# A two-layer decoder on one core: the order of a pair's sum on TensorE, GpSimd's additions, and the start of a recurrence

## The chip, the core and the metric

The kernel runs on one core of a Trainium2 chip. TensorE (PE) does matrix products and transposes into the PSUM banks, VectorE (DVE), ScalarE (ACT) and GpSimd (POOL) work on tiles of 128 partitions, and each engine goes through its own instructions in the order in which they are written. They wait for one another by semaphores. The metric is the time of one execution on the device in microseconds; less is better. It is given as the median of several runs.

## The reference

Input are x of 8 x 256 x 128 and a context of 8 x 512 x 128, in float32. Six blocks follow on each other, each with a residual and a layer norm:

```python
x = _layernorm(x + _L0_attn_ref(x, ...))    # 16 heads of 8; causal band of 64, relative bias
x = _layernorm(x + _L0_xattn_ref(x, ctx))   # 16 heads of 64; norms, rope on keys
x = _layernorm(x + _L0_ffn_ref(x, ...))     # ternary weights, activations scaled by a global max
x = _layernorm(x + _L1_attn_ref(x, ...))    # recurrence over the 256 positions
x = _layernorm(x + _L1_xattn_ref(x, ctx))   # linear attention, 16 heads of 8
x = _layernorm(x + _L1_ffn_ref(x, ...))     # fp8 quantised input and weights, + bias

# the two that the change touches most
attn = jnp.clip(einsum('bhnd,bhsd->bhns', q, rope(k)) * scale, -11.0, 11.0)
out = einsum('bhns,bhsd->bhnd', softmax(attn), v) @ Wo + bo
def step(state, inp):                       # 256 times
    u_t, sp_t = inp
    state = jnp.tanh(state @ A.T + u_t @ B.T) + sp_t
    return (state, state @ C.T)
```

## The kernel before

**Stages.** In a set-up of about 53 us the weights and the context are loaded and split, and the self attention of batch 0 is computed. The main loop follows: 8 batches, each of 8 pairs of cross-attention heads (p = 0 to 7). Beside a batch's pairs runs the self attention of the next batch, cut in 48 slots, six to a pair. A batch lasts 93 us; the first is shorter (part of its preparation lies in the set-up), as is the last (no self attention beside it). Then comes the quantised FFN's end and the start of the recurrence, the 255 steps of the recurrence with the linear attention of the second layer beside them, and a tail with the fp8 product and the last norm.

**Split numbers.** Matrix products of float32 inputs are made from a high and a low part (fp32r): three matmuls L1803, L1804, L1805 for each. The high part is a cast (L1340, L1342 for the weights' wq and wv in the set-up), the low part the difference (L1349).

**A pair.** The keys are turned by rope on VectorE (`keys_job("a")` makes k_cos, L1312; `keys_job("b")` makes k_sin, L1314) and added on GpSimd (`rotate`, L659, two pairs ahead). `unit(0)` and `unit(1)` on TensorE (L2204) make the scores of the pair in transposed form, half the context each. ScalarE takes the exponential (L1003), VectorE clamps it (`clamp`, L1499), which is the clip of the scores. `values_of` (L2113) multiplies the exponentials with the values. The denominator of the softmax takes two steps: GpSimd adds the four blocks of context positions (L752 when the first clamp is done, L758 and L759 when the second is; L759 gives `psum_ready`), and `sum_of` (L2124) adds over the partitions with a matmul of ones and gives `o_full`. On that VectorE's `attended` waits: a reciprocal (L1399), then the product (L1400). Values, sum and `attended` belong to the pair before.

**The order around the change** is written by hand for each engine. TensorE does unit(0), keys a, a slot, values and sum of the pair before, a slot, unit(1), queries, a slot, keys b, the rest:

```python
if pair >= 1:
    values_of(pair - 1)
    sum_of(pair - 1)
slots(1, 2)
unit(1)
```

VectorE does keys a, clamp(0), two slots, `attended(pair - 1)`, clamp(1), a slot, keys b, the other slots. GpSimd does two slots, L752, L758, L759, three slots, `rotate(pair + 2)`, a slot. Which work stands in which slot is a table: `S_X1` = 37 (the norm of x with b_wo added, L642 to L710) is in pair 6, `S_LATN`, `S_LAT` = 38, 43 make the latents of the next batch (L1187), `S_AFFINE` = (36, 38) multiplies the linear attention's keys by l_g and adds l_b (L696), `S_RELU` = 40 and the k, v product (L1933) follow. TensorE's row maxima for the self attention are made by VectorE (L1248, L1250) from the scores L1819.

**Start of the recurrence.** `begin_z(k)` (L2300, L2301) makes the input part of the first 32 steps for four batches in `cf`, with 256 and 252 columns for each k; step 0 is the first tanh (L1049). `quantize_weights` (L1486, L1487, L1423 to L1427) and the peak `f_peak` (L1557) are on VectorE before. In the steps, matmuls without use (`keep_clock`, L2130) fill TensorE where no other work stands.

**Tail.** `begin_sum(k)` (L2485) puts x5 and b_ffn, both times a diagonal, in a bank; the fp8 product (L2502) is added. ScalarE's `copy_q8` (L1096) brings the turned inputs, `normalize_last` (L1076) applies the last norm with rstd and tail_bias, which GpSimd makes (L818 to L821).

Of the kernel before, what the change touches and what calls it, by code (L numbers as in the profile page):

```python
# [23 lines left out]
ALU = mybir.AluOpType  # L24
# [44 lines left out]
S_AFFINE, S_RELU, S_KV_SUM = (36, 38), 40, 44  # L69
# [116 lines left out]
def decoder(nc, a, out):  # L186
    with ExitStack() as ctx:
# [3 lines left out]
        def sem(name):  # L191
            return ctx.enter_context(nc.semaphore(name))
# [6 lines left out]
        cf = sc[:, :, :].rearrange("p k c -> p (k c)")  # L199
        ob = ctx.enter_context(nc.psum_tensor("out_bank", [P, 512], F32))  # L200
# [130 lines left out]
        f_peak = sb("f_peak", [P, B - 1])  # L331
# [52 lines left out]
        x5_last = sem("x5_last")  # L384
        w_top_ready = sem("w_top_ready")
# [56 lines left out]
        weights_split = sem("weights_split")  # L442
        keys_split = sem("keys_split")
# [168 lines left out]
        def _(pool):  # L612
# [125 lines left out]
            def batch(b, last=False):  # L738

                for p in range(PAIRS):  # L740
# [6 lines left out]
                    slots(0, 2)  # L747
# [8 lines left out]
                    link(first)  # L756
                    pool.wait_ge(clamped, 2 * pair + 2)
# [51 lines left out]
            def affine_of(k, count=4):  # L809
# [9 lines left out]
                link(g.tensor_tensor(rstd[:, at], var_eps[:, at], minus_half[:, at], ALU.pow))  # L819
# [13 lines left out]
            rstd_of(late, 3, 3, EPS_LN, half=1)  # L833
            for k in range(3):
                affine_of(4 + k)
# [8 lines left out]
        def _(act):  # L844
# [127 lines left out]
            even_turn(8)  # L972
            keep_kv(0, 1)
            even_turn(10)
# [141 lines left out]
            copy_q8(2)  # L1116
            normalize_last(0)
            copy_q8(3)
# [4 lines left out]
        def _(dve):  # L1123
# [206 lines left out]
            def split_high(part):  # L1330
# [8 lines left out]
                if part == 2:  # L1339
                    last = w.tensor_copy(wq_s[:, 0, :], wq_nat)  # L1340
                if part == 3:
                    last = w.tensor_copy(wv_s[:, 0, :], wkv_nat[:, INNER:2 * INNER])  # L1342
                last.then_inc(weights_high, 1)

            def split_low(part):

                dve.wait_ge(weights_high, part + 1)
                full, t = ((wq_nat, wq_s), (wkv_nat[:, INNER:2 * INNER], wv_s))[part - 2]
# [19 lines left out]
            split_high(2)  # L1368
# [3 lines left out]
            split_high(3)  # L1372
# [1162 lines left out]
```

## Time and profile before

| | us |
|---|---|
| median of 3 runs | 1004.24 |
| lowest and highest | 1001.86, 1004.31 |
| the profiled execution | 998.63 |
| its span in the trace | 996.9 |
| a batch of the loop (batches 1 to 6) | 93.00 |
| last batch | about 78 |
| end of the loop to step 0 | about 22.5 |
| 255 steps | about 145.5 |
| tail | about 50 |

Over the span TensorE is busy in 908.7 us (91%), VectorE in 687.6 (69%), ScalarE in 504.6 (51%), GpSimd in 501.1 (50%). Of the chain of work that ended last TensorE holds 53% and VectorE 26%. In the timelines a row is a group of like instructions that follow each other, with the start of the first, the time they hold the engine, and in brackets the idle time before them with what ended it. Ends of matmuls are modelled, so the start of the next row says better how long a row took.

### The profile page before, as it was taken

How to read it: one execution, taken by the hardware profiler on the slowest of the kernel's cores; microseconds unless marked ns; L12 is line 12 of the kernel's file. 1: busy time of each engine (PE TensorE's matmuls, PEld its weight loads, DVE VectorE, ACT ScalarE, POOL GpSimd, SP SyncE). 2: the span in 40 equal slices, each digit the busy share in tenths (PEclk: the TensorE clock that was granted, in tenths of full speed). 3: DMA queues.
4: the chain of work that ended last, by engine and by line, in shares of the span. 5: the costliest groups of instructions: out<-in, count | busy, mean ns of one | idle time of the engine just before them, and what ended most of it. 6: DMA issues, size and time to landing. Idle time of an engine off the chain costs nothing.

```text
span 996.9 us, 22201 instructions
## 1 busy us (share of the span) xinstructions
PE 908.7 (91%) x8566; PEld 647.8 (65%) x8566; DVE 687.6 (69%) x1911; ACT 504.6 (51%) x1434; POOL 501.1 (50%) x635
## 2 busy tenths in 40 slices
PE   6679999999999999999999999999899499999944
PEld 4456657666666766666666666666666389998832
DVE  6866578568757875786688567857799735444476
ACT  6456636653764566456646654764243033333324
POOL 2654465367446645664565367456667112333352
PEclk9999999999999999999999999999999689999967
DMA  8000000000000000000000000000000002122111
GB/s 202 23 7 12 1 2 6 12 1 7 12 1 1 7 12 1 1 7 11 2 6 1 12 2 1 1 1 1 23 1 1 0 8 31 32 33 31 30 22 42
DMA packets 60470, 15.09 MB, mean 15 GB/s; under 512 B 41278, under 2 KB 59726, under 8 KB 60238
## 3 DMA queue, kind: packets, MB, share of 16 engines
q1 hardware_dynamic: 59822, 13.42, 6.4%
q8 instruction: 68, 1.11, 0.5%
q14 instruction: 36, 0.29, 0.1%
q10 hardware_dynamic: 544, 0.26, 0.1%
HBM read 10.51 MB, written 3.17 MB: 14 GB/s over the span
## 4 chain that ended last, share of the span: by engine, by line
PE 53%; DVE 26%; POOL 10%; ACT 6%; issue 4%; DMA 1%; POOLq 0%; DVEq 0%; SPq 0%; ACTq 0%
PE score_banks L2204 8%; DVE o_rec L1399 7%; PE out_bank L2113 6%; DVE prob L1499 6%; PE bank_a L1798 4%; PE score_banks L1803 4%; PE score_banks L2325 3%; PE score_banks L2130 3%; PE score_banks L1834 3%; POOL psum L758 3%; PE bank_d L2338 2%; POOL psum L759 2%; PE bank_d L1819 2%; PE score_banks L1804 2%; PE score_banks L1805 2%
## 5 line engine op out<-in xcount | busy, mean ns | idle before, releaser
L1003 ACT ACTIVATE prob<-score_banks 128x1024 f32<-128x1024 f32 x128 | 130.9, 1023 | 161.5 <-PE score_banks L2204 161.1
L758 POOL TENSOR_TENSOR psum<-psum,prob 128x512 f32<-128x512 f32 x63 | 80.4, 1276 | 140.6 <-DVE prob L1499 140.6
L2204 PE MATMUL score_banks<-qh,kr 64*128 64x256 f32 x1024 | 145.2, 402 | 2.8 <-ACT qh L935 1.9
L1399 DVE RECIPROCAL o_rec<-out_bank 128x256 f32<-128x256 f32 x64 | 111.8, 1747 | 23.5 <-PE out_bank L2124 23.4
L752 POOL TENSOR_TENSOR psum<-prob 128x512 f32<-128x512 f32 x64 | 82.6, 1290 | 89.9 <-DVE prob L1499 89.8
L2113 PE MATMUL out_bank<-prob,v 128*64 128x256 f32 x1024 | 124.7, 385 | 0.5 <-DVE on L1400 0.5
L2204 PEld LDWEIGHTS score_banks<-qh,kr 64*128 64x128 f32 x1024 | 88.7, 186 | 39.9 <-issue 30.6
L1499 DVE TENSOR_SCALAR prob<-prob 128x1024 f32<-128x1024 f32 x128 | 101.4, 793 | 12.5 <-ACT prob L1003 12.5
L886 ACT ACTIVATE prob<-prob,neg_max 128x128 f32<-128x128 f32 (+1 forms) x256 | 107.1, 427 | 5.5 <-DVE neg_max L1255 5.5
L2113 PEld LDWEIGHTS out_bank<-prob,v 128*64 128x64 f32 x1024 | 67.7, 136 | 45.8 <-issue 17.2
L1052 ACT ACTIVATE prob<-score_banks 128x8 f32<-128x8 f32 x255 | 45.2, 177 | 93.3 <-PE score_banks L2325 93.3
L759 POOL TENSOR_TENSOR psum<-psum,prob 128x512 f32<-128x512 f32 x63 | 80.3, 1275 | 4.9
L659 POOL TENSOR_TENSOR kr<-k_cos,k_sin 128x512 f32<-128x512 f32 x64 | 81.5, 1273 | 1.8 <-DVE k_sin L1314 1.1
L2325 PE MATMUL score_banks<-prob,pt 128*64 128x8 f32 x1020 | 73.9, 210 | 0.3 <-ACT prob L1049 0.3
L1312 DVE TENSOR_TENSOR k_cos<-score_banks,cos_t 128x512 f32<-128x512 f32 x56 | 38.0, 679 | 44.4 <-PE score_banks L1805 27.2
L854 ACT ACTIVATE pt<-bank_a 128x512 f32<-128x512 f32 x84 | 50.2, 598 | 35.5 <-PE bank_a L1798 34.6
L2325 PEld LDWEIGHTS score_banks<-prob,pt 128*64 128x64 f32 x1020 | 51.5, 135 | 16.1 <-ACT prob L1052 8.4
L2130 PE MATMUL score_banks<-w_qkv_t,ident 128*64 128x96 f32 (+1 forms) x336 | 60.7, 264 | 0.0
L1798 PE MATMUL bank_a<-ident,prob 128*128 128x128 f32 x360 | 56.9, 280 | 4.2 <-ACT pt L854 2.3
L1834 PE MATMUL score_banks<-pt,vm 128*32 128x128 f32 x768 | 54.0, 281 | 5.3 <-ACT pt L940 2.6
L1819 PE MATMUL bank_d<-km,q 64*128 64x128 f32 x480 | 49.2, 322 | 9.1 <-DVE row_max L1250 7.2
L784 POOL TENSOR_TENSOR var_eps<-mv,epsilons 128x1 f32<-128x1 f32 x49 | 10.2, 209 | 93.4 <-DVE mv L1616 93.3
(440 smaller groups left out, 2132.6 us busy)
## 6 DMA issues: line engine op xcount, KB each, us to landing
cb<-in_ctx_dram SPq DMA_DIRECT2D x8, 256.0 KB, 2.8
bias_mask<-bias_scratch SPq DMA_DIRECT2D x4, 384.0 KB, 5.2
xb<-in_x_dram SPq DMA_DIRECT2D x8, 128.0 KB, 2.1
prob<-in_L_xattn_Wkv_dram SPq DMA_DIRECT2D x1, 1024.0 KB, 9.7
x_scratch<-v SPq DMA_DIRECT2D x16, 64.0 KB, 1.5
bias_mask<-x_scratch SPq DMA_DIRECT2D x16, 64.0 KB
att_scratch<-on SPq DMA_DIRECT2D x16, 64.0 KB, 1.5
prob<-att_scratch SPq DMA_DIRECT2D x16, 64.0 KB, 3.0
```

Of the source, the lines that this page charges most:

```text
L758: link(g.tensor_tensor(psum[:, p % 2, :], psum[:, p % 2, :], pp[:, 2, :], ALU.add))
L759: g.tensor_tensor(psum[:, p % 2, :], psum[:, p % 2, :], pp[:, 3, :], ALU.add).then_inc(psum_ready, 1)
L886: last = s.activation(pr, pr, ACT.Exp, bias=neg_max[:, qt, j, g:g + 1], accum_out=row_sum[:, qt, j, g:g + 1])
L1003: s.activation(prob[:, p % 2, 2 * u:2 * u + 2, :].rearrange("p k (h q) -> p h k q", h=2), sc[:, 0:2, :].rearrange("p h (k q) -> p h k q", ...
L1399: link(w.reciprocal(o_rec[:, :], bank[:, T:2 * T]))
L1499: w.tensor_scalar(pr, pr, float(np.exp(-CLIP)), float(np.exp(CLIP)), ALU.max, ALU.min).then_inc(clamped, 1)
L1798: return nc.tensor.transpose(out_ap, in_ap, ident[0:in_ap.shape[0], 0:in_ap.shape[0]])
L1834: last = mm(o0_bank[32 * g:32 * g + 32, qt * P:(qt + 1) * P], vm[:, kt, j, 32 * g:32 * g + 32], pt[:, t % 2, i * P:(i + 1) * P], start=(j ...
L2113: mm(o[DH * h:DH * (h + 1), 0:T], v[:, (q // 2) % 2, kb, lo:lo + DH], prob[:, q % 2, kb, T * h:T * (h + 1)], start=(kb == 0), stop=(kb == ...
L2130: mm(bank[0:HALF_ROWS, 0:columns], ident[:, 0:HALF_ROWS], w_qkv_t[:, 0:columns], start=True, stop=True, skip_group_check=True)
L2204: last = mm(sc[:, h, k * T:(k + 1) * T], kr[rows_of, p % 2, kb * P:(kb + 1) * P], qh[rows_of, p % 2, :], start=True, stop=True, skip_group ...
L2325: last = mm(cf[lo:lo + HALF_ROWS, t * B:(t + 1) * B], a_t[:, lo:lo + HALF_ROWS], hid[:, (t - 1) * B:t * B], start=False, stop=True, skip_g ...
```

## The change

- **Sum.** In each pair TensorE does `sum_of(pair - 1)` behind `unit(1)`, no longer right behind the values.
- **GpSimd.** The multiplication by l_g is in slot 34 (pair 5) instead of 36; in pair 6 the first addition goes ahead of slot 37.
- **Set-up.** The high parts of wv and wq are made by ScalarE; VectorE makes their low parts in other places; keys a of pair 1 come behind the latents' slot.
- **Start of the recurrence.** Before step 0 only the first 16 steps get their input part, in the bank `bank_d2` (`z_of`); the next 16 steps' part is made in steps 1 to 8, by two matmuls in a step (`next_z`), and `keep_clock` gets 96 columns there. `quantize_weights` comes later, the peak is taken by batches.
- **Tail.** For k = 0, 1 GpSimd adds b_ffn to x5 beforehand, and `begin_sum` needs one term. The last three biases are one instruction of VectorE (`bias_of`) in place of two of GpSimd. `copy_q8(3)` comes ahead of `normalize_last(0)`.

```diff
-S_AFFINE, S_RELU, S_KV_SUM = (36, 38), 40, 44
+S_AFFINE, S_RELU, S_KV_SUM = (34, 38), 40, 44
...
# GpSimd, a pair
-                    slots(0, 2)
+                    early = 1 if p == S_X1 // PER_PAIR else 2
+                    slots(0, early)
                     pool.wait_ge(clamped, 2 * pair + 1)
...
                     link(first)
+                    slots(early, 2)
                     pool.wait_ge(clamped, 2 * pair + 2)
...
# ScalarE, set-up
             even_turn(8)
+            act.wait_ge(split_in, 16 * 2)
+            s.activation(wv_s[:, 0, :], wkv_nat[:, INNER:2 * INNER], ACT.Identity).then_inc(values_high, 1)
+            s.activation(wq_s[:, 0, :], wq_nat, ACT.Identity).then_inc(values_high, 1)
+            even_turn(10)
             keep_kv(0, 1)
-            even_turn(10)
...
# VectorE, set-up
             self_attention(0, S_CN_LOW, 0)
-            split_high(2)
             odd_turn(7)
             keep_cos()
             measure_kv(0, 1)
-            split_high(3)
-            split_low(2)
             odd_turn(9)
             invert_sums(0)
             odd_turn(11)
+            split_low(0)
             self_attention(0, S_DIVIDE, 0)
-            split_low(3)
...
             first_keys("b", 0)
+            split_low(1)
             self_attention(0, S_LATN, 0)
+            self_attention(0, S_LAT, 0)
             first_keys("a", 1)
-            self_attention(0, S_LAT, 0)
...
# TensorE, a pair
                     if pair >= 1:
                         values_of(pair - 1)
-                        sum_of(pair - 1)
                     slots(1, 2)
                     unit(1)
+                    if pair >= 1:
+                        sum_of(pair - 1)
...
# TensorE, start of the recurrence
+            pe.wait_ge(y_free, B)
...
-                zv, xv = (t[:, 0:Z_FIRST].rearrange("p (t b) -> p t b", b=B)[:, :, batches] for t in (cf, x3_t))
+                zv, xv = (t[:, 0:P].rearrange("p (t b) -> p t b", b=B)[:, :, batches] for t in (bank_d2, x3_t))
                 mm(zv, bwi_t, xv, start=False, stop=False, skip_group_check=True)
-                return mm(zv[:, 1:], aws_t, xv[:, 0:Z_FIRST // B - 1], start=False, stop=True, skip_group_check=True)
+                return mm(zv[:, 1:], aws_t, xv[:, 0:WINDOW_STEPS - 1], start=False, stop=True, skip_group_check=True)
+
+            def next_z(at):
+
+                k, at = divmod(at, 4)
+                second, half = divmod(at, 2)
+                of = halves[half]
+                batches = slice(4 * k, 4 * k + 4)
+                lag = B if second else 0
+                weights = (bwi_t, aws_t)[second]
+                mm(cf[of, P:Z_FIRST].rearrange("p (t b) -> p t b", b=B)[:, :, batches], weights[:, of],
+                   x3_t[:, P - lag:Z_FIRST - lag].rearrange("p (t b) -> p t b", b=B)[:, :, batches], start=False,
+                   stop=True, skip_group_check=True)
...
# tail: ScalarE, TensorE
             copy_q8(2)
+            copy_q8(3)
             normalize_last(0)
-            copy_q8(3)
...
-                for rhs, first in ((x5[:, 4 * k:4 * k + 4, :], True),
-                                   (b_ffn[:, :].unsqueeze(1).broadcast_to([P, 4, D]), False)):
+                if k < 2:
+                    pe.wait_ge(x5b_ready, k + 1)
+                terms = [((x2, x5)[k // 2][:, 4 * k:4 * k + 4, :], True)]
+                if k >= 2:
+                    terms.append((b_ffn[:, :].unsqueeze(1).broadcast_to([P, 4, D]), False))
+                for rhs, first in terms:
```

The line numbers move: what was L2113, L2124, L2204 and L1803 is L2142, L2153, L2233 and L1831 in the changed kernel. On TensorE, in pair 3 of a batch, before (each row is one instruction with its output and inputs; `x4` means four alike):

```order
776 L1834 MATMUL score_banks<-pt,vm 32x128 x4
777 L2113 MATMUL out_bank<-prob,v 64x256 x8
778 L2124 MATMUL out_bank<-psum,ones 64x256 x2
779 L2204 MATMUL score_banks<-qh,kr 128x256 x4
780 L1803 MATMUL score_banks<-lat_s,wq_s 128x256
```

and in the changed kernel:

```order
776 L1862 MATMUL score_banks<-pt,vm 32x128 x4
777 L2142 MATMUL out_bank<-prob,v 64x256 x8
778 L2233 MATMUL score_banks<-qh,kr 128x256 x4
779 L2153 MATMUL out_bank<-psum,ones 64x256 x2
780 L1831 MATMUL score_banks<-lat_s,wq_s 128x256
```

The sum, out_bank from psum and ones, has gone from between values and scores to behind the scores.

On GpSimd, from pair 5's last two additions to pair 6's, before:

```order
81 L759 TENSOR_TENSOR psum<-psum,prob 128x512
82 L659 TENSOR_TENSOR kr<-k_cos,k_sin 128x512
83 L642 TENSOR_TENSOR var_eps<-mv,epsilons 128x2
84 L644 TENSOR_TENSOR rstd<-var_eps,minus_half 128x2
85 L696 TENSOR_TENSOR k<-k,l_g 128x512
86 L642 TENSOR_TENSOR var_eps<-mv,epsilons 128x2
87 L644 TENSOR_TENSOR rstd<-var_eps,minus_half 128x2
88 L710 TENSOR_TENSOR x<-x,b_wo 128x256
89 L752 TENSOR_TENSOR psum<-prob 128x512
90 L758 TENSOR_TENSOR psum<-psum,prob 128x512
```

and in the changed kernel:

```order
81 L768 TENSOR_TENSOR psum<-psum,prob 128x512
82 L703 TENSOR_TENSOR k<-k,l_g 128x512
83 L666 TENSOR_TENSOR kr<-k_cos,k_sin 128x512
84 L649 TENSOR_TENSOR var_eps<-mv,epsilons 128x2
85 L651 TENSOR_TENSOR rstd<-var_eps,minus_half 128x2
86 L760 TENSOR_TENSOR psum<-prob 128x512
87 L649 TENSOR_TENSOR var_eps<-mv,epsilons 128x2
88 L651 TENSOR_TENSOR rstd<-var_eps,minus_half 128x2
89 L717 TENSOR_TENSOR x<-x,b_wo 128x256
90 L767 TENSOR_TENSOR psum<-psum,prob 128x512
```

The multiplication by l_g stands ahead of the rotation of pair 5, and the first addition of pair 6 (psum from prob alone) ahead of the second rstd and x.

## Rows read from the trace of the kernel before

**Rows 1.** Stages: length, busy PE, PEld, DVE, ACT, POOL, clock, DMA, GB/s
```profile
329.10:422.10 93.00, 89.55 (x693) 60.80 (x692) 67.00 (x175) 53.53 (x136) 51.51 (x53) 1.00 0.02 6
701.00:779.00 78.00, 70.02 (x506) 47.71 (x505) 67.80 (x131) 26.04 (x37) 50.97 (x51) 1.00 0.03 8
779.00:801.50 22.50, 12.91 (x41) 9.16 (x41) 14.73 (x58) 2.83 (x4) 3.82 (x7) 0.58 0.00 0
```

**Rows 2.** Waits of PE, five batches, 220 to 686: total, times, longest
```profile
PE out_bank L2124 <- POOL psum L759: 5.8, 5, 1.2
PE bank_d L1819 <- DVE row_max L1250: 4.2, 5, 0.9
```

**Rows 3.** Waits of DVE in the same stretch
```profile
DVE o_rec L1399 <- PE out_bank L2124: 15.6, 15, 1.4
```

**Rows 4.** Timeline of PE, batch 3, pairs 2 and 3: start, length
```profile
362.68 0.82 PE L1819 MATMUL bank_d<-km,q 64*128 64x128 f32 x8
...
369.20 1.95 PE L2113 MATMUL out_bank<-prob,v 128*64 128x256 f32 x16
370.97 0.60 PE L2124 MATMUL out_bank<-psum,ones 128*64 128x256 f32 x4
371.51 1.13 PE L2204 MATMUL score_banks<-qh,kr 64*128 64x256 f32 x8
372.57 0.39 PE L1803 MATMUL score_banks<-lat_s,wq_s 128*128 128x256 f32 x1
...
376.54 0.38 PE L1803 MATMUL score_banks<-wv_s,cn_s 128*128 128x256 f32 x1 [0.24 <-DVE k_sin L1314]
```

**Rows 5.** Timeline of DVE, batch 3, pairs 1 to 3
```profile
347.73 1.75 DVE L1399 RECIPROCAL o_rec<-out_bank 128x256 f32<-128x256 f32 x1
...
358.66 1.76 DVE L1399 RECIPROCAL o_rec<-out_bank 128x256 f32<-128x256 f32 x1 [0.39 <-PE out_bank L2124]
...
371.62 1.76 DVE L1399 RECIPROCAL o_rec<-out_bank 128x256 f32<-128x256 f32 x1 [1.36 <-PE out_bank L2124]
...
375.81 0.68 DVE L1314 TENSOR_TENSOR k_sin<-score_banks,sin_t 128x512 f32<-128x512 f32 x1
```

**Rows 6.** Timeline of all engines, batch 2, pair 7
```profile
318.94 1.03 ACT L1003 ACTIVATE prob<-score_banks 128x1024 f32<-128x1024 f32 x1 [1.27 <-PE score_banks L2204]
...
319.95 1.58 DVE L1187 TENSOR_SCALAR lat<-x,mv,rstd 128x128 f32<-128x128 f32 x2
320.17 1.28 POOL L758 TENSOR_TENSOR psum<-psum,prob 128x512 f32<-128x512 f32 x1 [0.69 <-DVE prob L1499]
...
322.85 0.65 PE L2124 MATMUL out_bank<-psum,ones 128*64 128x256 f32 x4 [1.17 <-POOL psum L759]
...
324.05 1.48 DVE L1261 TENSOR_SCALAR k<-k 128x512 f32<-128x512 f32 x1 [1.92 <-POOL k L696]
```

**Rows 7.** Timeline of DVE, set-up, 31 to 49
```profile
31.78 1.76 DVE L1340 CAST wq_s<-prob 128x1024 fp32r<-128x1024 f32 x1
...
35.87 0.66 DVE L1342 CAST wv_s<-prob 128x1024 fp32r<-128x1024 f32 x1
36.44 1.22 DVE L1349 TENSOR_TENSOR wq_s<-prob,wq_s 128x1024 fp32r<-128x1024 f32 x1
...
42.47 1.36 DVE L1349 TENSOR_TENSOR wv_s<-prob,wv_s 128x1024 fp32r<-128x1024 f32 x1
...
48.56 0.60 DVE L1187 TENSOR_SCALAR lat<-x,mv,rstd 128x128 f32<-128x128 f32 x2 [0.51 <-POOL rstd L644]
```

**Rows 8.** Timeline before step 0, PE and ACT
```profile
797.80 1.06 PE L2300 MATMUL score_banks<-prob,pt 128*128 128x256 f32 x2
798.05 1.09 ACT L986 ACTIVATE prob<-out_bank 128x512 f32<-128x512 f32 x1 [0.77 <-PE out_bank L1798]
```

**Rows 9.** Timeline of the tail, PE and ACT
```profile
978.41 1.86 PE L2485 MATMUL bank_d<-b_ffn,q 128*128 128x512 f32 x2
...
988.96 0.61 ACT L1096 ACTIVATE q_t<-bank_a 128x512 bf16<-128x512 bf16 x1
```

More of the change, by code:

```diff
@@ L199, in decoder, with z_of @@
         cf = sc[:, :, :].rearrange("p k c -> p (k c)")
+        def z_of(t, count=1):
+            return (bank_d2 if t < WINDOW_STEPS else cf)[:, t * B:(t + count) * B]
         ob = ctx.enter_context(nc.psum_tensor("out_bank", [P, 512], F32))
@@ L330, in decoder @@
         peak = sb("peak", [P, 5])
-        f_peak = sb("f_peak", [P, B - 1])
+        f_peak = sb("f_peak", [P, B])
         tail_bias = sb("tail_bias", [P, 8])
@@ L818, in affine_of @@
                 link(g.tensor_tensor(var_eps[:, at], mv[:, at, 1], eps, ALU.add))
-                link(g.tensor_tensor(rstd[:, at], var_eps[:, at], minus_half[:, at], ALU.pow))
+                last = g.tensor_tensor(rstd[:, at], var_eps[:, at], minus_half[:, at], ALU.pow)
+                if k >= 4:
+                    last.then_inc(rstd_ready, 1)
+                    return
+                link(last)
                 link(g.tensor_tensor(tail_bias[:, at], mv[:, at, 0], rstd[:, at], ALU.mult))
@@ L833, in _ @@
             rstd_of(late, 3, 3, EPS_LN, half=1)
+            pool.wait_ge(red_ready, 3)
+            for k in range(2):
+                part = slice(4 * k, 4 * k + 4)
+                g.tensor_tensor(x2[:, part, :], x5[:, part, :], b_ffn[:, :].unsqueeze(1).broadcast_to([P, 4, D]),
+                                ALU.add).then_inc(x5b_ready, 1)
             for k in range(3):
@@ L1338, in split_high @@
                                              wkv_nat[:, 0:INNER].rearrange(swapped, t=2, d=HALF)[:, 1 - t])
[L1339 to L1342, printed above, removed]
                 last.then_inc(weights_high, 1)
             def split_low(part):
-                dve.wait_ge(weights_high, part + 1)
-                full, t = ((wq_nat, wq_s), (wkv_nat[:, INNER:2 * INNER], wv_s))[part - 2]
+                dve.wait_ge(values_high, part + 1)
+                full, t = ((wkv_nat[:, INNER:2 * INNER], wv_s), (wq_nat, wq_s))[part]
                 w.tensor_tensor(t[:, 1, :], full, t[:, 0, :].bitcast(F32), ALU.subtract).then_inc(weights_split, 1)
@@ L1554, in _ @@
             normalize_f(B - 1)
-            quantize_weights()
+            find_f_peak(B - 2)
             dve.wait_ge(f_t_free, B)
-            link(w.tensor_reduce(f_peak[:, B - 2:B - 1], f_t[:, (B - 2) * T:B * T], AX_X, ALU.max,
+            link(w.tensor_reduce(f_peak[:, B - 1:B], f_t[:, (B - 1) * T:B * T], AX_X, ALU.max,
                                  apply_absolute_value=True))
@@ L1763, in measure_sum, with bias_of @@
                 measure(tiles_of_sum(k), k % 2)
+            def bias_of(k):
+                at = slice(4 * (k % 2), 4 * (k % 2) + 4)
+                dve.wait_ge(rstd_ready, late + 5 + k)
+                w.scalar_tensor_tensor(out=tail_bias[:, at], in0=mv[:, at, 0], scalar=-1.0, in1=rstd[:, at],
+                                       op0=ALU.mult, op1=ALU.mult).then_inc(tail_bias_ready, 1)
             quantize(0)
@@ L1770, in _ @@
             measure_sum(1)
+            bias_of(0)
             measure_sum(2)
+            bias_of(1)
             def measure_tiles(lo, at):
@@ L2324, in step @@
                 for lo in range(0, P, HALF_ROWS):
-                    last = mm(cf[lo:lo + HALF_ROWS, t * B:(t + 1) * B], a_t[:, lo:lo + HALF_ROWS],
+                    last = mm(z_of(t)[lo:lo + HALF_ROWS], a_t[:, lo:lo + HALF_ROWS],
                               hid[:, (t - 1) * B:t * B], start=False, stop=True, skip_group_check=True)
```

32 lines of the change are left out of this document (22 added, 10 removed).

## The prediction

> **What bounds the kernel now.** The view by stages says where the time is: a batch of the main loop lasts 93.00 us and TensorE is busy in 89.55 of it [rows 1]; the other seven batches are like it, except the first (about 76 us, since its early work lies in the set-up) and the last, where TensorE is busy in 70.02 of 78.00 us. So TensorE bounds the loop, and all its gaps in a batch come to 3.4 us. The reader is to see two things in that: no edit that only takes TensorE's gaps away can bring more than 3.4 us a batch, and there is almost no air to take up a delay. The waits of five batches say what ends those gaps: 5.8 us in 5 times at the sum L2124 behind GpSimd's L759, 4.2 us in 5 times at L1819 behind the row maxima [rows 2]. The first is what the change aims at: 1.17 us once per batch, in pair 7. Then I asked the other way round who waits for the sum. VectorE's reciprocal waited 15.6 us in 15 times for L2124 [rows 3], three times per batch. So in three pairs of eight the sum is not an idle appendix of the values, but the step that lets VectorE go on.
>
> The timelines of TensorE and VectorE through batch 3 say what hangs on that. In pair 3 the sum starts at 370.97 and the next scores at 371.51; the reciprocal starts at 371.62 after 1.36 us of idleness, and VectorE then works without a break (reciprocal, product, clamp, four row maxima, their negation, k_sin from 375.81 for 0.68); TensorE's next keys start at 376.54, 0.24 us late, behind that k_sin [rows 4, 5]. The path sum, VectorE, TensorE is therefore the bound there.
>
> **Part 1, the sum behind the second scores.** In each pair but the first, the four sum matmuls go behind unit(1), eight score matmuls. TensorE does them at 371.51 and goes on at 372.57 by the chain of starts, so 1.06 us [rows 4]. Nothing is added to TensorE's work but one more change of tile shape: the sum has the same tiling as the values before it (its four start 0.11 apart, like the values' sixteen in 1.77), and from the sum's start to the scores it is 0.54, 0.10 more than four times 0.11 [rows 4]. The sum now stands between two other tilings, so that change comes once more, and I count 0.15 with the longer first group. The sum ends 1.06 + 0.15 = 1.21 us later against the values.
>
> The Trainium skill has a rule on this ("TensorEngine Tiling (Array Packing)", section Key Properties): changing the tiling mode drains TensorE. The trace agrees with a small price, the 0.10 above; it is a rule that speaks against this order.
>
> By pairs, what is late next:
> - Pair 3: VectorE's chain binds, as shown. It starts 1.21 later, TensorE's wait of 0.24 becomes 1.45: +1.21.
> - Pair 2: the reciprocal starts at 358.66, 0.39 us after VectorE was free, behind the sum; product, clamp and four row maxima follow (in pair 3 the like takes 3.8 from the reciprocal's start), so the maxima end near 362.5, and TensorE's L1819, which needs them, starts at 362.68 [rows 4, 5]. The slack is about 0.15. So +1.06 for the delay less that slack, and 0.15 for the switch, about +1.16.
> - Pair 1: the reciprocal starts at 347.73, when VectorE comes free and not when the sum is done [rows 5]. By the order of the rows the moved sum ends some 0.2 to 0.3 after that, and the chain ends in TensorE's wait of 0.86 at L1819 behind row maxima (4.2 in 5 times [rows 2]), which grows by it: +0.35.
> - Pair 0: as pair 1, but behind the product stand the output matmuls of the batch before, at the end of the pair, which follow at once. I take 0.3 for the delay and 0.15 for the switch, near pair 1's: +0.45.
> - Pairs 4 and 5: the reciprocal comes later, but TensorE does not wait for VectorE soon after; the switch alone, +0.15 each.
>
> **Part 2, GpSimd's order in pairs 5 to 7.** The multiplication by l_g goes from pair 6 into pair 5 ahead of the rotation, and the first addition L752 ahead of the pair-6 slot with x1. In pair 7 the 1.17 us at the sum [rows 6] go: GpSimd comes to its additions earlier, and the sum asks later by 1.06. But what is late next is the latents' normalisation: VectorE's two operations take 1.58 us together from 319.95 while L758 runs on GpSimd from 320.17 to 321.45, against 0.33 for an undisturbed one (the second ends when L758 ends), and the relu that follows took 1.48 from 324.05 under L696 and L659, after a wait of 1.92 for l_b [rows 6]. The k, v product of TensorE waits for that relu. Behind the change the l_g and the first additions meet the same VectorE operations in other places: in pair 5 the rotation is 1.27 later, and k_cos of pair 6 waits for it. I estimate +1.4 for these against −1.17, so +0.2 for pairs 6 and 7 together, with −0.65 if nothing of it blocks.
>
> The page "SBUF — State Buffer" of the Trainium skill (section SBUF: two separate sides) says that VectorE and GpSimd share a port pair that one instruction holds alone to its end. Rows 6 agree: the stretched operations end with GpSimd's.
>
> The sum of a batch: 0.45 + 0.35 + 1.16 + 1.21 + 0.15 + 0.15 + 0.2 = +3.7, bounds +2.3 (pairs 2 and 3 and the switches, pairs 0 and 1 absorbed, −0.65) and +4.2. Six such batches +22.1; batch 0 has no sum in its first pair and less self attention to wait for, +3.1; in the last batch four of the sums release a reciprocal on the path, about +4.1. **Together +29.3**.
>
> **Part 3, the set-up.** Ahead of VectorE's reciprocals of the row sums, three operations leave: 1.76 (wq_s), 0.66 (wv_s), and the low part 1.22; the low part of 1.36 between o and y leaves too [rows 7]. On the other side the wq low part, 1.22, goes in ahead of the latents' normalisation with 0.51 us of idleness as cover [rows 7]. VectorE's chain to the first scores is shorter by 1.76 + 0.66 + 1.22 + 1.36 − 0.71 = 4.3. ScalarE does the two conversions in their place (a 128x1024 operation of it takes 1.03 [rows 6]), in a hole of its own before keep_kv; I charge 0.3. **−4.0**, bounds −2.5 (ScalarE's hole is not where I put it) and −4.6.
>
> **Part 4, the start of the recurrence.** TensorE's four matmul pairs of 256 and 252 columns at half the clock begin at 797.80, 0.85 apart, and become 64 and 60 columns. The second half of them can't begin before ScalarE's copy from 798.05 ends, 1.09 later [rows 8], so 1.5 comes off, not 2.5. The recurrence then starts in the half clock (0.58 granted in that stage [rows 1]); its first eight steps carry the other 384 columns as extra matmuls, about 0.8 us together. f_peak comes 0.57 earlier because the weights' quantisation moves behind, where VectorE waits anyway; this is half lost to ScalarE. **−1.3**, bounds −2.2 and 0.
>
> **Part 5, the tail.** The first of the b_ffn matmul pairs, 1.86 at half the clock [rows 9], goes, but what follows waits for q8; −1.2. copy_q8(3), which stood behind the normalisation until 988.96 [rows 9], comes some 2.8 earlier, the bias path on GpSimd is two operations of 0.20 shorter, but the end then hangs on the statistics and the power on GpSimd in series: −0.3 to −0.7. **−1.5**, bounds −1.9 and +1.0: TensorE gets its full clock back near 980 after a stretch with this very work; with less of it the later matmul pairs may run at 1.2 GHz.
>
> **Sum.** 29.3 − 4.0 − 1.3 − 1.5 = +22.5. The profiled execution took 998.63 us, the median of the three runs is 1004.24, 0.6% above; the change by the sum is the same against either: 1021.1 on the profile's basis, **1026.7** on the median's.
>
> **The rivals.**
> 1. The forecast: the delayed sum is on VectorE's path in pairs 2 and 3 and partly in 0 and 1. Chance 0.68.
> 2. The same mechanism, but pairs 0 and 1 take up their delay and nothing blocks in pairs 6 and 7: +2.3 a batch, over the loop 6 x 2.3 + 2 + 3.5 = +19, less 6.8: 1016. For it speaks that VectorE is busy in only 67.00 of 93.00 us [rows 1]. 0.15.
> 3. The other side: the delay of the sum is taken up everywhere. Place: pair 3's k_sin and pair 2's row maxima. It decides at whether VectorE's chain behind the sum still ends before TensorE gets there; it would have to be 1.2 us shorter, for instance because the product and reciprocal no longer meet GpSimd's operations. Then only the switch costs, 8 x 0.15 = 1.2 a batch, and the wait of 1.17 goes: 0 a batch. The other stages give −6.8, and a part of the L1819 waits may go with it, 2 more: 995 to 997. Against it: the idle 1.36 us before the reciprocal and the idle 0.24 before the keys, with nothing free between [rows 4, 5]. 0.12.
> 4. That the start and the tail lose their clock: the forecast's loop, +3: 1030. 0.05. It is in the range.
>
> **How the numbers follow.** About 0.3%, 3 us, is what a measurement of this kernel can tell from no change. Rivals 1, 2 and 4 are slower by more, 0.68 + 0.15 + 0.05 = 0.88; of rival 3 0.12, faster; between them some lands within 3 us, for which I move 0.04 from the slower side and 0.01 from the faster: faster 0.11, same 0.05, slower 0.84. The range: the forecast's own bounds are +2.3 to +4.2 a batch over eight batches, about +19 to +33, less 8.7 to 2, so 1014 to 1035; with 2 us for the spread of the median the low end is 1012, which leaves out rival 3 and the ends. High 1034.
>
> **What would show it.** In pair 3 of a batch VectorE's idleness before the reciprocal should be about 2.4 (before 1.36 plus the scores), and TensorE's wait at the value keys L1831 (the old L1803) behind k_sin about 1.4, five times in five batches. The sum's wait for GpSimd should be gone. A batch should last about 96.7. The first scores should begin near 48.9 instead of 52.89. I am wrong if a batch lasts 93 or less: then VectorE's chain after the sum was not the bound, or GpSimd's new order gives it more than I see. I am wrong on part 2 if the wait at the k, v product does not show.

## The result, and the profile after

| | before | after |
|---|---|---|
| median (4 runs each) | 1003.05 us | 1024.58 us |
| lowest and highest | 1001.12, 1004.31 | 1023.06, 1026.19 |
| ratio, 95% interval | | 1.0235 [1.0213, 1.0258] |
| the profiled execution | 998.63 | 1025.33 |

The changed kernel is slower by 2.35% in the recorded ratio. Its two medians lie 21.5 us apart, which is 2.15%; in the sets of runs behind the experiments the kernel before had medians of 1000.0 to 1001.3, and against these the change costs 23 to 25 us. The two profiled executions lie 26.7 us apart; that of before is below all its timed runs, and that of after in the upper half of its. By the starts of score rows and of tanh rows the 26.7 us divide like this:

| stretch | before | after | difference |
|---|---|---|---|
| start to the first scores | 52.89 | 49.75 | −3.14 |
| batches 0 to 6 | 648.04 | 673.11 | +25.07 |
| first scores of batch 7 to the last scores' last row | 68.34 | 72.61 | +4.27 |
| from there to the tanh of step 0 | 32.17 | 32.05 | −0.12 |
| 255 steps | 145.53 | 147.78 | +2.25 |
| last tanh to the end | 49.94 | 48.31 | −1.63 |

The loop has lost 29.3 us. The stage view of one batch of after, with the columns of [rows 1], and the start of the recurrence (this second row begins 5.5 us behind the last scores, its counterpart in [rows 1] 9.7 us, so their lengths can't be compared; both end at step 0):

```profile
336.30:432.90 96.60, 90.60 (x691) 60.18 (x690) 66.00 (x174) 54.60 (x136) 52.40 (x53) 1.00 0.02 5
801.00:827.50 26.50, 14.03 (x57) 10.65 (x57) 19.70 (x72) 3.36 (x4) 4.23 (x8) 0.61 0.00 0
```

TensorE is busy in 90.60 us where it was 89.55, and has 6.0 us of gaps where it had 3.4: 1.0 of the 3.6 us that a batch has grown is more busy time of TensorE (eight more changes of tile shape at 0.15 would be 1.2), 2.6 is waiting. What the waiting is for stands in TensorE's waits of five batches (in total, times, longest), and below it VectorE's first row:

```profile
PE bank_d L1847 <- DVE row_max L1274: 9.9, 10, 1.1
PE score_banks L1831 <- DVE k_sin L1338: 6.8, 5, 1.4
PE bank_d L1961 <- DVE k L1285: 5.3, 5, 1.1
PE out_bank L2142 <- DVE on L1418: 1.8, 5, 0.4
```

```profile
DVE o_rec L1417 <- PE out_bank L2153: 48.9, 30, 3.4
```

The sum no longer waits for GpSimd ([rows 2] had 5.8 us for that), but the row maxima have gone from 4.2 us in 5 times to 9.9 in 10, and k_sin from 0.24 a batch to 1.37. VectorE waits 9.8 us a batch for the moved sum, in six pairs, where it waited 3.1 in three [rows 3]. The length of such a wait doesn't say what it costs: the longest, 3.4 us, stands in pair 5, which grew by 0.15, and that of 2.6 in pair 3, which grew by 1.2.

In pair 2 of batch 3 the chain of waits shows one such turn from TensorE to VectorE and back:

```profile
366.19 1.06 PE score_banks L2233 x8
367.25 0.61 PE out_bank L2153 x4
367.86 0.02 issue
367.88 1.77 DVE o_rec L1417
369.65 0.02 issue
369.67 0.42 DVE on L1418
370.10 0.60 DVE prob L1517
...
371.68 0.14 issue
371.82 0.82 PE bank_d L1847 x8
```

Values, scores, sum, reciprocal, product, clamp, row maxima, TensorE: the scores L2233 have come to stand in this chain; before, they ran beside it. In pair 3 the timelines of VectorE and TensorE answer to [rows 5] and [rows 4]:

```profile
381.97 1.76 DVE L1417 RECIPROCAL o_rec<-out_bank 128x256 f32<-128x256 f32 x1 [2.58 <-PE out_bank L2153]
```

```profile
386.88 0.38 PE L1831 MATMUL score_banks<-wv_s,cn_s 128*128 128x256 f32 x1 [1.37 <-DVE k_sin L1338]
```

Idle 2.58 instead of 1.36 before the reciprocal, and 1.37 instead of 0.24 before the keys: about 1.2 more at either end. Pair by pair, from one pair's first scores to the next pair's in batch 3 (starts of the L2204 or L2233 rows in the trace of each kernel):

| pair | 0 | 1 | 2 | 3 | 4 | 5 | 6 | 7 | batch |
|---|---|---|---|---|---|---|---|---|---|
| before | 12.04 | 12.38 | 12.40 | 14.85 | 11.20 | 11.94 | 6.84 | 11.32 | 92.96 |
| after | 12.49 | 12.74 | 13.53 | 16.06 | 10.99 | 12.09 | 6.73 | 12.00 | 96.63 |
| sum's order alone (e1) | 12.49 | 12.74 | 13.54 | 16.04 | 10.98 | 12.09 | 6.73 | 11.73 | 96.33 |
| all but the sum's order (e2) | 12.03 | 12.38 | 12.40 | 14.84 | 11.20 | 11.94 | 6.84 | 10.81 | 92.45 |
| e2 without GpSimd's order (e6) | 12.03 | 12.38 | 12.41 | 14.84 | 11.20 | 11.94 | 6.84 | 11.34 | 92.99 |
| sum moved in pairs 4 to 7 (e4) | 12.04 | 12.39 | 12.40 | 14.84 | 10.99 | 12.08 | 6.73 | 11.99 | 93.47 |
| after, half reciprocal (e3) | 12.02 | 11.95 | 12.73 | 15.27 | 10.98 | 12.09 | 6.73 | 10.90 | 92.67 |
| e2, half reciprocal (e8) | 11.88 | 11.81 | 12.39 | 14.85 | 11.20 | 11.94 | 6.84 | 10.51 | 91.43 |

### The profile page after: what moved, and what is told of

It reads as the page before. It is cut to its first block, busy times and chain, and to the rows that moved or that the text cites. A ratio compares the mean times of both kernels' runs of the same rounds, so it can differ in the third digit from the quotient of the medians.

```text
span 1023.6 us, 22230 instructions
## 1 busy us (share of the span) xinstructions
PE 919.3 (90%) x8580; PEld 647.7 (63%) x8580; DVE 679.5 (66%) x1913; ACT 515.0 (50%) x1436; POOL 508.4 (50%) x631
## 3 DMA queue, kind: packets, MB, share of 16 engines
q8 instruction: 69, 1.13, 0.5%
HBM read 10.51 MB, written 3.17 MB: 13 GB/s over the span
## 4 chain that ended last, share of the span: by engine, by line
PE 60%; DVE 24%; POOL 8%; issue 3%; ACT 3%; DMA 1%; POOLq 0%; DVEq 0%; SPq 0%; ACTq 0%
PE score_banks L2233 10%; DVE o_rec L1417 9%; PE out_bank L2142 8%; PE bank_a L1826 4%; PE score_banks L1831 4%; PE score_banks L2159 3%; PE score_banks L2369 3%; PE score_banks L1862 3%; DVE prob L1517 3%; PE out_bank L2153 3%; PE out_bank L2125 3%; PE bank_d L2382 2%; POOL psum L767 2%; PE bank_d L1847 2%; POOL k L703 2%
## 5 line engine op out<-in xcount | busy, mean ns | idle before, releaser
L767 POOL TENSOR_TENSOR psum<-psum,prob 128x512 f32<-128x512 f32 x63 | 80.6, 1279 | 182.6 <-DVE prob L1517 182.6
L2233 PE MATMUL score_banks<-qh,kr 64*128 64x256 f32 x1024 | 145.5, 402 | 1.6 <-ACT prob L1024 1.0
L2142 PE MATMUL out_bank<-prob,v 128*64 128x256 f32 x1024 | 124.6, 385 | 4.0 <-DVE on L1418 4.0
L2233 PEld LDWEIGHTS score_banks<-qh,kr 64*128 64x128 f32 x1024 | 88.4, 186 | 39.0 <-issue 29.1
L2142 PEld LDWEIGHTS out_bank<-prob,v 128*64 128x64 f32 x1024 | 67.7, 136 | 49.8 <-issue 14.7
L1517 DVE TENSOR_SCALAR prob<-prob 128x1024 f32<-128x1024 f32 x128 | 87.7, 685 | 3.6 <-ACT prob L1024 3.6
L1073 ACT ACTIVATE prob<-score_banks 128x8 f32<-128x8 f32 x240 | 42.7, 178 | 87.0 <-PE score_banks L2369 87.0
L2369 PE MATMUL score_banks<-prob,pt 128*64 128x8 f32 x960 | 69.3, 210 | 0.0
L947 ACT ACTIVATE v<-score_banks 128x512 f32<-128x512 f32 x57 | 34.1, 598 | 67.5 <-PE score_banks L1833 66.8
L793 POOL TENSOR_TENSOR var_eps<-mv,epsilons 128x1 f32<-128x1 f32 x49 | 10.4, 211 | 93.1 <-DVE mv L1635 93.0
L2369 PEld LDWEIGHTS score_banks<-prob,pt 128*64 128x64 f32 x960 | 48.3, 134 | 12.9 <-ACT prob L1073 6.5
```

Source lines behind the costliest of these rows:

```text
L767: link(g.tensor_tensor(psum[:, p % 2, :], psum[:, p % 2, :], pp[:, 2, :], ALU.add))
L1517: w.tensor_scalar(pr, pr, float(np.exp(-CLIP)), float(np.exp(CLIP)), ALU.max, ALU.min).then_inc(clamped, 1)
L2142: mm(o[DH * h:DH * (h + 1), 0:T], v[:, (q // 2) % 2, kb, lo:lo + DH], prob[:, q % 2, kb, T * h:T * (h + 1)], start=(kb == 0), stop=(kb == ...
L2233: last = mm(sc[:, h, k * T:(k + 1) * T], kr[rows_of, p % 2, kb * P:(kb + 1) * P], qh[rows_of, p % 2, :], start=True, stop=True, skip_group ...
L2369: last = mm(z_of(t)[lo:lo + HALF_ROWS], a_t[:, lo:lo + HALF_ROWS], hid[:, (t - 1) * B:t * B], start=False, stop=True, skip_group_check=True)
```

## Experiments

The theory (A): the moved sum lets VectorE's reciprocal begin 1.2 us later, and where TensorE soon needs what VectorE makes behind it, the delay comes back to TensorE. The rivals: GpSimd's moved operations cost (B), or the additional change of tile shape does (C).

**e1, the sum's order alone.** The kernel before with

```diff
                         values_of(pair - 1)
-                        sum_of(pair - 1)
                     slots(1, 2)
                     unit(1)
+                    if pair >= 1:
+                        sum_of(pair - 1)
```

> The kernel before with one edit: on TensorE the sum of a pair stands behind the next pair's unit(1). Theory A (the sum lets VectorE's reciprocal start, and VectorE's chain from there sets the end in pairs 0 to 3): a batch grows by what the changed kernel shows in its pairs 0 to 5 (0.46 + 0.36 + 1.13 + 1.21 - 0.21 + 0.16 = 3.1 us) less the 1.17 of the sum's wait for GpSimd in pair 7, which goes, so by 2 to 3.1 us, 16 to 25 in all. Rival B (the moved GpSimd work in pairs 5 to 7 is what costs): a batch falls by up to 1.2, the whole by up to 8 us. Rival C (only one more change of tile shape per pair): 8 x 0.15 less 1.17, no change.

Measured: 1027.38 us against 1001.33, ratio 1.0266 [1.0246, 1.0286]. This edit by itself costs as much as the whole change and somewhat more; pairs 0 to 6 are those of after within 0.02 us. B falls as the main cause, and C at the price that it was given; that a change of tile shape costs more than that is left to e3. The cost came out above what I expected for A: 3.4 us a batch instead of 2 to 3.1 and 26.1 in all instead of 16 to 25, because pair 7 got longer (11.73 against 11.32) where I had let it gain.

**e2, all but the sum's order.**

> The changed kernel with the sum right behind the values again; GpSimd's order, the set-up, the start of the recurrence and the tail stay changed. Theory A: pairs 0 to 3 last as before (12.04, 12.38, 12.40, 14.85 us), the first scores begin 3.1 us earlier, the tail is 1.6 shorter, steps and start between -2 and +2; pairs 6 and 7 decide the rest, between -1.2 and +0.6 a batch: 992 to 1004 us in all. Rival B (GpSimd's moved work costs): a batch stays at 95 to 96.6, 1015 to 1022 us.

Measured: 990.81, ratio 0.9899 [0.9879, 0.9920]: everything else in the change together is a gain of 1%, and the time lies below the 992 that I had given as the lower end. Pairs 0 to 6 are back to before. Pair 7 takes 10.81, less than before, so GpSimd's new order is good when the sum stands in its old place. Put the other way, the sum's order costs 1.0235 against 0.9899, about 34 us on top of the rest, and 26 alone: the difference of about 8 us is mostly pair 7, where the move costs 1.19 a batch with GpSimd's new order and 0.4 with its old, 5.5 us over seven batches.

**e3, half the reciprocal, in the changed kernel.** Reciprocal and product as

```diff
-                link(w.reciprocal(o_rec[:, :], bank[:, T:2 * T]))
+                link(w.reciprocal(o_rec[:, 0:P], bank[:, T:T + P]))
```

with the product reading the 128 columns twice; half of the reciprocals are left out, and half of the heads are divided by the wrong sums. The reciprocal took 0.96 us instead of 1.76, so 0.80 less, not the 0.88 that I expected.

> The changed kernel with the reciprocal over 128 of the 256 columns of the sums (the other heads' queries are divided by the wrong sums, so part of the softmax's division is left out); about 0.88 us less of VectorE's work per pair behind the moved sum, TensorE's work untouched. Theory A: the delays of pairs 0 to 3 shrink by up to 0.88 each and the waits that were there before too, so a batch falls from 96.65 to 93.5 to 94.3, the whole by 18 to 24 us. Rival C (the loss is TensorE's, from the extra change of tile shape or contention in the bank): a batch keeps 96.2 or more, the whole falls by 3 us at most.

Measured: 989.65, ratio 0.9887 [0.9867, 0.9906], 35 us below after, a batch of 92.67 instead of 96.63. TensorE's instructions are the same as in after, so the 4 us a batch were VectorE's, and pairs 1, 2 and 3 fell by the whole 0.80 (−0.79, −0.80, −0.79). The fall was larger than my expectation of A (18 to 24): I had counted pairs 0 to 3 (pair 0 gave −0.47), not pair 7 (−1.10) and the last batch (−5.6, with 1.3 of it a fall of the clock in after).

**e8, the same with the sum in its old place**, a single run.

> The kernel of e2 with the reciprocal over 128 of 256 columns, as in e3 (part of the softmax's division is left out). In e3 0.88 us less of VectorE's work in a pair took 3.96 off a batch. Theory A (VectorE is on the path behind the moved sum, and hardly otherwise): here it takes off at most what TensorE waits for row maxima and k_sin, 0.85 + 0.24 = 1.1 a batch: 91.3 to 92.3 us. Rival (VectorE is the bound in either order): about 4 off here too, 88.5.

Measured: 979.18, a batch of 91.43, so 1.0 less than e2, as A had it. The same 0.80 us less of VectorE's work in each pair is worth 4.0 us a batch behind the moved sum and 1.0 behind the old one. It is the plainest sign of what the change did: behind the moved sum VectorE's chain was on the path in five pairs, 0 to 3 and 7.

**e4, the sum moved in pairs 4 to 7 only.**

```diff
+                    if pair >= 1 and p < 4:
+                        sum_of(pair - 1)
                     slots(1, 2)
                     unit(1)
-                    if pair >= 1:
+                    if pair >= 1 and p >= 4:
                         sum_of(pair - 1)
```

> The changed kernel with the sum behind unit(1) only in pairs 4 to 7 of a batch; in pairs 0 to 3 it stands right behind the values. Theory A: pairs 0 to 3 are as before the change, pairs 4 to 7 as after it (-0.21, +0.16, -0.11, +0.66): a batch of 93.5 us, 25 to 26 less 4: the whole at 1002 to 1005 us. Rival (the delay is passed on from pair to pair, so that the late pairs lose what the early ones gain): a batch of 95 or more.

Measured: 999.68, ratio 0.9993 [0.9981, 1.0005], a batch of 93.47. The batch came as expected, the whole lies 2.3 us below the 1002 that I had given as the lower end. The pairs add up: each pair's price belongs to its own sum and isn't passed on. Pair 7 keeps its 11.99. What it waits for in after is in the timelines of batch 2, GpSimd, VectorE and TensorE:

```profile
327.31 1.31 POOL L767 TENSOR_TENSOR psum<-psum,prob 128x512 f32<-128x512 f32 x1 [0.95 <-DVE prob L1517]
...
329.93 1.27 POOL L703 TENSOR_TENSOR k<-k,l_b 128x512 f32<-128x512 f32 x1
```

```profile
327.15 1.56 DVE L1211 TENSOR_SCALAR lat<-x,mv,rstd 128x128 f32<-128x128 f32 x2
...
331.24 1.48 DVE L1285 TENSOR_SCALAR k<-k 128x512 f32<-128x512 f32 x1 [1.93 <-POOL k L703]
```

```profile
326.69 1.95 PE L2142 MATMUL out_bank<-prob,v 128*64 128x256 f32 x16 [0.36 <-DVE on L1418]
328.86 0.41 PE L1826 MATMUL bank_a<-ident,lat 128*128 128x128 f32 x2 [0.22 <-DVE lat L1211]
...
332.87 1.13 PE L1961 MATMUL bank_d<-v,k 128*128 128x130 f32 x8 [1.06 <-DVE k L1285]
```

The latents' normalisation again runs beside L767 and takes 1.56 for two, the relu again 1.48 beside l_b and the rotation; and the k, v product now waits 1.06 for that relu. The sum's wait for GpSimd (1.17 before) has moved to the product behind it, and two small waits (0.36 and 0.22) have come to it. That wait of the product comes with the moved sum and not with GpSimd's new order: in e1, which has the old one, it is the same, 5.3 us in five batches.

**e6, GpSimd's order as before**, the rest as e2.

> The kernel of e2 with GpSimd's order as before (l_g in pair 6, first addition behind slot 37). Theory A: pair 7 takes 11.3 us again instead of 10.81 and the sum waits 1.17 instead of 0.66 for GpSimd; a batch is 0.5 longer, 3.7 us in all: 993 to 996 us. Rival: GpSimd's move brings nothing by itself and pair 7 stays at 10.8.

Measured: 994.52, ratio 0.9951 [0.9934, 0.9967], pair 7 at 11.34. GpSimd's order by itself is worth 0.53 a batch, 3.7 us. It was in the change to no use, since with the moved sum pair 7 is 12.00 with it (after) and 11.73 without (e1).

**e11, the set-up alone**, the kernel before with the edits of ScalarE, VectorE and TensorE in the set-up.

> The kernel before with the set-up's edits alone. By the changed kernels' first scores, at 48.9 to 50.6 us instead of 52.9 and 54.9, the whole gets 3 to 4 us faster: 996.5 to 998.5. Rival (what the set-up gains is lost before the second batch): no change.

Measured: 995.02, ratio 0.9946 [0.9934, 0.9959], so 5 us, somewhat more than I expected; the first scores at 49.73.

**e5, the kernel of e2 with the sum moved in pair 4 alone, and with the start of the recurrence as before.** Of its edit the part on the sum, against the kernel before:

```diff
                         values_of(pair - 1)
-                        sum_of(pair - 1)
+                        if p != 4:
+                            sum_of(pair - 1)
                     slots(1, 2)
                     unit(1)
+                    if p == 4:
+                        sum_of(pair - 1)
```

> The kernel of e2 (changed, the sum behind the values) with two edits: in pair 4 alone the sum goes behind unit(1), and all 32 steps' input part is made before step 0 again, as in the kernel before. In e4 pair 4 lasted 10.99 us against 11.20 in e2 and pair 5 12.08 against 11.94. If the 0.14 of pair 5 belongs to its own moved sum, a batch is 0.21 shorter, 1.5 us in all; if it is passed on from pair 4, it is 0.07. Old start: the first 16 steps take 8.7 to 9.4 us, as in the kernel before and in e1, instead of 10.5, and step 0 comes 1 us later: between -1.5 and 0. Together 988 to 991 us.

Measured: 989.31, ratio 0.9884 [0.9866, 0.9903]. Pair 4 took 10.98 and pair 5 11.94: the gain of 0.2 is real and isn't passed on. The change of tile shape costs what I had counted (values 1.88 instead of 1.78 to the next start, sum 0.58 instead of 0.53), but behind it three distances from one group's start to the next are shorter than in e2, by 0.20, 0.05 and 0.13 us. What TensorE had waited for there isn't shown. The other half of the expectation was wrong: with the old start, the first 16 steps still took 10.57 us, as in e2 (10.50) and not as in before (9.36). The stage view shows the clock at half until 4.8 us after its step 0, which was at 795.44:

```profile
799.00:800.00 1.00, 1.00 (x11) 0.84 (x10) 0.00 (x0) 0.18 (x1) 0.00 (x0) 0.50 0.00 0
800.00:801.00 1.00, 1.00 (x13) 0.69 (x10) 0.00 (x0) 0.25 (x2) 0.00 (x0) 0.86 0.00 0
```

So the slow steps aren't the new start's doing alone. That it makes them likelier isn't excluded: without filling, the half clock ended 3.4 to 6.7 us after step 0 in all six kernels with the new start, and at −1.0 (e1), −1.0 (e11), 1.2 (before) and 4.8 (e5) with the old.

**e7, TensorE kept busy before step 0.** The kernel of e2 with

```diff
+            pe.wait_ge(f_t_free, B)
+            for _ in range(6):
+                keep_clock(KEEP, bank_a)
             turn_x3(0)
```

> The kernel of e2 with six matmuls without use (192 columns each) on TensorE in the idle 3.4 us ahead of the turns of x3. Theory D (the steps after step 0 are slow because TensorE did too little before, so that its clock rose late): full clock is granted earlier than 3.5 us after step 0, as in the kernel before (1.2 us), and the first 16 steps take 8.7 to 9.4 instead of 10.5: -1 to -2 us. Rival: the additional matmuls of the steps themselves make the difference; then nothing changes.

Measured: 989.19, ratio 0.9890 [0.9868, 0.9912], 1.6 below e2 in the medians and within their intervals. The granted clock (the last column but two) from step 0 on in after and in e2, and around step 0 in e7:

```profile
827.52:833.52 6.00, 5.77 (x53) 4.74 (x53) 0.00 (x0) 1.25 (x7) 0.00 (x0) 0.50 0.01 3
833.52:839.00 5.48, 5.46 (x92) 4.81 (x92) 1.81 (x8) 1.60 (x9) 0.00 (x0) 0.95 0.00 0
```

```profile
793.20:797.20 4.00, 3.72 (x36) 2.98 (x37) 0.00 (x0) 0.89 (x5) 0.00 (x0) 0.57 0.00 0
```

```profile
784.00:786.00 2.00, 2.00 (x8) 1.36 (x7) 1.93 (x11) 0.00 (x0) 1.00 (x2) 0.50 0.00 0
786.00:791.90 5.90, 3.67 (x24) 2.68 (x22) 5.26 (x22) 2.22 (x2) 1.43 (x3) 1.00 0.01 1
791.90:801.00 9.10, 8.85 (x140) 7.34 (x142) 2.61 (x11) 2.83 (x16) 0.00 (x0) 1.00 0.01 2
```

In after the 6.6 us from step 0 on ran at 1.2 GHz, in e2 the first 3.4; in e7 the clock was 2.4 GHz from 786 on, 5.9 us ahead of step 0, and the first 16 steps took 9.20 instead of 10.50. In this execution theory D held.

**e9, the best of these**: e7 with the sum moved in pair 4.

> The kernel of e7 (changed, the sum right behind the values, six idle-filling matmuls before the turns of x3), and in pair 4 of a batch the sum behind unit(1) as in e5. By the pairs of e5 pair 4 lasts 10.98 us instead of 11.20 and the other pairs stay, in the last batch pair 5 is about 1 us longer: -0.2 x 7 + 1.1, so nothing to -0.5 us against e7: 987 to 991 us.

Measured: 987.87, ratio 0.9875 [0.9861, 0.9889]: 12 us below before. It is the fastest here that leaves nothing out (e8 is faster, without half of the reciprocals), though the intervals of e5, e7 and e10 overlap with its own. But its steps weren't those of e7:

```profile
788.00:792.70 4.70, 2.39 (x17) 1.86 (x16) 4.11 (x15) 2.21 (x2) 1.01 (x1) 1.00 0.01 2
792.70:796.70 4.00, 3.73 (x38) 3.15 (x38) 0.83 (x4) 0.89 (x6) 0.00 (x0) 0.59 0.00 0
796.70:803.00 6.30, 6.28 (x104) 5.34 (x103) 1.75 (x7) 1.95 (x11) 0.00 (x0) 0.99 0.01 3
```

With the same six matmuls the clock was at 2.4 GHz 6.1 us ahead of step 0 (5.9 in e7, 6.2 in e10, and at most 1.0 in the ten kernels without them), but from 0.7 us after step 0 on it was at half again for 3.4 us (0.59 in the second row), and the first 16 steps took 1.2 us longer than in e7. The filling gives full clock before step 0, but not surely behind it.

**e10, the same with TensorE kept busy before the tail.**

```diff
+            pe.wait_ge(ta_free, ja)
+            for _ in range(14):
+                keep_clock(KEEP, bank_a)
             pe.wait_ge(td_free, jd)
```

> As e9, with fourteen more matmuls without use (192 columns) on TensorE in its 7.7 us of idleness ahead of the tail's peak. Theory D (the clock is high where TensorE was busy before): the first two pairs of sums L2535, about 1.9 and 1.3 us at the half clock, run at the full one, and the product of the fp8 inputs comes sooner: the tail, 48.0 to 48.3 us from the last tanh, is 0.5 to 1.5 shorter. Rival: VectorE's quantisation sets the tail's pace, and the clock changes nothing.

Measured: 988.49, ratio 0.9892 [0.9873, 0.9911], no gain over e9; the tail is 48.01 us, e2's was 48.02.

```profile
960.00:965.00 5.00, 2.92 (x18) 2.02 (x16) 3.74 (x13) 1.65 (x4) 2.58 (x7) 1.00 0.00 0
965.00:968.00 3.00, 1.24 (x3) 0.79 (x4) 2.21 (x10) 1.77 (x3) 1.95 (x2) 0.68 0.00 0
968.00:971.00 3.00, 3.00 (x8) 1.00 (x7) 2.78 (x5) 2.00 (x5) 0.00 (x0) 0.50 0.02 5
```

The clock came up where nothing needed it and was at half again from 966.1 to 972.9. The first two pairs of sums, at which the filling was aimed, started at 967.1 and 969.6, so they ran at the half clock as in e2. The rival isn't shown by that either: whether VectorE sets the tail's pace stays open.

## Why the prediction was right, point by point

The forecast was 1026.7 with 1012 to 1034, the measured median is 1024.58. What was forecast is a difference, +22.5; measured are 21.5 by the medians, 23.6 by the recorded ratio and 26.7 between the profiled executions. The terms can be compared only with these last, so they miss by +4.2 together, which the medians don't show. By the terms of the sum:

- **Pairs 0 to 3.** Forecast +0.45, +0.35, +1.16, +1.21; measured +0.45, +0.36, +1.13, +1.21. The +1.16 of pair 2 doesn't come out of the working: 1.06 less the slack of 0.15 and 0.15 for the switch is 1.06. e1, e3 and e8 show the mechanism too: VectorE's chain behind the sum. The signs named beforehand came as well: idleness before pair 3's reciprocal about 2.4 (2.58), the wait behind k_sin about 1.4 (1.37), a batch near 96.7 (96.6). The first scores came at 49.75, not near 48.9.
- **Pairs 4 and 5.** Forecast +0.15 each, measured −0.21 and +0.15. The step on pair 4 failed: the switch costs 0.15 there too, but 0.38 us between the starts behind it went with it (e5).
- **Pairs 6 and 7.** Forecast +0.2 together, measured −0.11 and +0.68, so +0.57. The path was right (the latents and the relu beside GpSimd's operations, then the k, v product), its size by 0.4 too small: I had let the gain of 1.17 stand in full, while the product's wait for the relu took 1.06 of it. It was wrong to put this down to GpSimd's new order, since e1 has the same wait without it. The wait of k_cos for the rotation did grow as forecast, from 9.7 us in 5 times to 18.9 in 10 over five batches, but TensorE paid nothing for it: pair 6 takes 6.73 in after and in e1.
- **The loop.** Forecast +29.3, measured 25.07 + 4.27 = 29.3. The errors in pair 4 and in pair 7 cancelled each other, so the agreement of the sum is better than that of its terms. Luck has a second part in it: in batch 7 pair 3 took 12.41 us in after against 11.13 in e1 (10.05 before), and the 1.28 between them are a fall of the clock in this one execution, behind a wait of 1.99 for k_sin: from there to the next scores TensorE took 2.86 us, in e1 1.58. Without it the last batch had been +3.0, where +4.1 was forecast.

```profile
762.40:765.80 3.40, 3.40 (x14) 3.03 (x16) 3.37 (x9) 1.03 (x2) 3.32 (x4) 0.50 0.00 0
```

- **The set-up.** Forecast −4.0, measured −3.14 from the profile's start. But the work itself began later in the execution of after; from the context's low part to the first scores it is 23.87 us before and 19.92 after, −3.95. VectorE's low part of the context, with which this count begins, before, then after, where the reciprocals of the row sums follow without the three operations of [rows 7] ahead of them:

```profile
29.02 2.84 DVE L1302 TENSOR_TENSOR cn_s<-k_sin,cn_s 128x512 fp32r<-128x512 f32 x1
```

```profile
29.83 2.84 DVE L1326 TENSOR_TENSOR cn_s<-k_sin,cn_s 128x512 fp32r<-128x512 f32 x1
...
35.57 1.75 DVE L1242 RECIPROCAL row_rec<-row_sum 128x128 f32<-128x128 f32 x2
```

- **The start of the recurrence.** Forecast −1.3, measured −0.12 before step 0 and +2.25 in the steps, +2.1 in all. This is the step that failed. Its 0.8 stood for the extra matmuls of the first steps, and nothing was put down for a half clock that lasts longer than before: it ended 1.2 us after step 0 before and 6.6 after. The extra matmuls themselves cost some 0.2: at full clock the first 16 steps took 9.20 in e7 and 9.04 in e1 and e11, which don't have them. By e5 the long half clock isn't a property of the changed start alone. The −1.3 isn't the sum of its terms either: −1.5, +0.8 and half of −0.57 make −1.0. The −0.12 is likely two things, as far as one profile of each kernel can tell: from the last scores to step 0 e2 takes 31.05, 1.1 less than before, and the moved sum adds 1.0 (e2 to after) or 0.7 (before to e1). From the last scores to the last tanh the kernels with the old start and the old order of the sum took 177.7 (before), 176.7 (e11) and 178.2 (e5), those with the new 177.7 (e2) and 177.1 (e6): the smaller first part brought nothing that these can tell.
- **The tail.** Forecast −1.5, measured −1.63. The stay of the clock at 1.2 GHz that I had feared for the later sums came for one matmul only, the first of the second pair (0.83 us to the next start against 0.48 before); the pairs from the third on ran 0.9 us each, as before.

The rival of the other side, that the delay is taken up, is refuted by pairs 2 and 3. The rival with +2.3 a batch is refuted by pairs 0 and 1. The fourth rival, that start and tail lose their clock, came true for the start in the profiled execution: the start of the recurrence and the steps are 3.4 us worse than forecast, and they make most of the 4.2 by which the profiles' difference exceeds the sum. How often the timed runs met it isn't known.

## What to carry to other kernels

Before moving a step behind other work because it waits for something, look at who waits for the step: the 1.17 us once a batch in front of the sum were visible, but behind the sum stood three waits of VectorE a batch, 3.1 us, and one of them led straight back to TensorE. A step that takes 0.5 us and releases another engine's chain belongs as early as its input allows, pair by pair if need be; the same move was worth −0.2 in pair 4 and +1.2 in pair 3. Gains that come with one bad edit are hidden by it: the rest of this change was worth 1%, and only taking the edits apart showed it.

## What the runs showed of the hardware that I had not expected

TensorE's clock around step 0 differs between kernels that are the same there: the first 16 steps took 9.0 to 9.4 us in before, e1, e7 and e11, 10.4 to 10.6 in e2, e3, e5, e6, e9 and e10, and 11.6 to 11.7 in after, e4 and e8. Apart from e5 the last two groups have the same instructions in these steps, and so has e7 of the first. In e9 and e10 the clock was up before step 0 and fell to 1.2 GHz for 3.4 us from 0.7 us behind it. Ahead of that fall TensorE was busy in 2.39 of 4.70 us in e9; e7, which kept its clock, had been busy in 3.67 of 5.90. Such falls came in the loop and the set-up too. In e5 one came in batch 7, behind a wait of 1.61 us and at the output matmuls, and pair 0 took 13.66 us instead of 12.03; e2 had the same wait and kept its clock. In after one came in pair 3 of batch 7, which cost 1.3. In e1 the clock was at half from 40.4 to 47.2 us, and the first scores came at 54.93 instead of 52.89, though TensorE had been busy in 1.66 of the 4.40 us ahead of it and before, which kept its clock, in 1.57. Why it falls in one kernel and not in another stays open.
